# Six-stage transformer block on one core: normalisation, gate and dispatch taken chunk by chunk into the end of the preceding stage

## The reference

```python
x = x + 0.5 * _L0_ffn_ref(_layernorm(x), ...)     # routed attention of top-k tokens, "ffn"
x = x + _L0_attn_ref(_layernorm(x), ...)          # causal attention, 16 heads of 8, "attn"
x = x + 0.5 * _L0_ffn_ref(_layernorm(x), ...)     # "ffn"
x = x + 0.5 * _L1_ffn_ref(_layernorm(x), ...)     # mixture of 8 experts, top 2, "moe"
x = x + _L1_attn_ref(_layernorm(x), ...)          # linear attention with a convolution, "lin"
x = x + 0.5 * _L1_ffn_ref(_layernorm(x), ...)     # "moe"

def _layernorm(x, eps=1e-05):
    return (x - mean(x)) / sqrt(var(x) + eps)

def _L1_ffn_ref(x, ln_w, Wg, bg, ...):
    xn = x * rsqrt(mean(x * x) + finfo.eps) * ln_w
    vals, idx = top_k(xn @ Wg + bg, 2)
    w = softmax(vals)
    # for each expert e: y = (silu(xn @ W1a + b1a) * (xn @ W1b + b1b)) @ W2 + b2
    # out = sum over the token's two experts of w * y
```

## Time and profile before

| what | value |
| --- | --- |
| median of three runs | 1043.1 us (1043.07 to 1043.85) |
| the profiled execution | 1034.16 us, span 1032.4 us |
| mean granted TensorE clock | 0.822 of full speed |
| busy PE, DVE, ACT, POOL | 671.4, 546.3, 388.5, 291.3 us |
| chain that ended last | PE 49%, DVE 23%, issue 7%, POOL 7%, ACT 6%, DMA 6% |
| of it the dispatch (POOL xg L485) | 6% |
| VectorE's scaled rows (L575) | 96 of 345 ns, 25.5 us |
| stage borders in the profile, about | 166, 396, 550, 766 and 818 us |

### The profile page before, as it was taken

The page is one execution under the profiler, slowest core; times in us unless marked ns, Lnnn a source line. Parts: engine busy times, 40 slices in busy tenths (PEclk is TensorE's granted clock), DMA queues, the critical chain, the costliest instruction groups (busy, mean ns, idle before and its releaser), DMA issues.

```text
span 1032.4 us, 13439 instructions
## 1 busy us (share of the span) xinstructions
PE 671.4 (65%) x4584; PEld 489.6 (47%) x4590; DVE 546.3 (53%) x1578; ACT 388.5 (38%) x689; POOL 291.3 (28%) x319
## 2 busy tenths in 40 slices
PE   2069895316999993079894029999715540899991
PEld 1056783211222232056784028999614430799990
DVE  6976758920111118976758404444388860344444
ACT  3053312425999983053311004444303020344440
POOL 2160202201223223060200742333307047133331
PEclk8579997756999997579995559999957855899996
DMA  9600000355510000000000244666220011566743
GB/s 347 231 1 1 1 1 15 81 95 107 67 23 1 2 2 1 0 1 1 1 2 0 85 151 139 211 216 197 89 81 0 1 52 64 194 197 210 218 142 132
DMA packets 40368, 86.74 MB, mean 84 GB/s; under 512 B 5592, under 2 KB 24664, under 8 KB 39784
## 3 DMA queue, kind: packets, MB, share of 16 engines
q1 hardware_dynamic: 35304, 75.53, 25.1%
q0 software_dynamic: 4992, 10.30, 2.8%
HBM read 70.93 MB, written 23.00 MB: 91 GB/s over the span
## 4 chain that ended last, share of the span: by engine, by line
PE 49%; DVE 23%; issue 7%; POOL 7%; ACT 6%; DMA 6%; SPq 3%; POOLq 0%; ACTq 0%; DVEq 0%
PE ps L1654 16%; PE ps L1665 8%; POOL xg L485 6%; PE ps L1568 4%; ACT arena L1255 4%; PE ps L1345 3%; DVE arena L584 2%; DVE arena L589 2%; PE ps L1551 2%; DMA arena<-scr_k 2%; SPq L334 2%; PE ps L1318 2%; DVE stats L514 2%; PE ps L1415 2%; PE ps L1452 1%
## 5 line engine op out<-in xcount | busy, mean ns | idle before, releaser
L845 DVE SCALAR_TENSOR_TENSOR arena<-ps,arena 128x256 f32<-128x256 f32 x184 | 89.1, 484 | 166.1 <-ACT arena L1286 166.1
L1654 PE MATMUL ps<-arena 128*128 128x256 f32 x736 | 170.6, 385 | 2.8 <-issue 1.5
L1255 ACT ACTIVATE arena<-ps 128x512 f32<-128x512 f32 (+3 forms) x192 | 138.4, 826 | 28.4 <-PE ps L1551 27.0
L1654 PEld LDWEIGHTS ps<-arena 128*128 128x128 f32 x736 | 138.2, 193 | 22.5 <-issue 4.0
L1286 ACT ACTIVATE arena<-ps,arena 128x256 f32<-128x256 f32 x184 | 87.5, 476 | 147.7 <-issue 89.9
L492 POOL DMA_INDIRECT yd<-arena x92 | 88.0, 957 | 188.3 <-DVE arena L853 174.2
L485 POOL DMA_INDIRECT xg<-Xn,arena x64 | 61.6, 963 | 106.8 <-DVE arena L781 87.9
L1665 PE MATMUL ps<-arena 128*128 128x128 f32 x736 | 89.8, 274 | 1.4 <-DVE arena L853 1.4
L1665 PEld LDWEIGHTS ps<-arena 128*128 128x128 f32 x736 | 86.0, 192 | 1.8 <-issue 1.7
L1568 PE MATMUL ps<-arena 128*32 128x512 f32 (+3 forms) x768 | 83.5, 507 | 2.4 <-DVE arena L1053 1.6
L474 POOL TENSOR_SCALAR_AFFINE_SELECT arena<-arena 128x512 f32<-128x512 f32 x64 | 40.6, 635 | 140.3 <-ACT arena L1255 140.3
(11 more groups left out here) (243 smaller groups left out, 1188.9 us busy)
## 6 DMA issues: line engine op xcount, KB each, us to landing
arena<-in_wall SPq DMA_DIRECT2D x46, 836.0 KB, 4.9
xg<-in_zeros SPq DMA_DIRECT2D x16, 520.0 KB, 15.8
arena<-xg SPq DMA_DIRECT2D x46, 130.0 KB, 3.9
arena<-yd SPq DMA_DIRECT2D x8, 512.0 KB, 5.6
arena<-scr_q SPq DMA_DIRECT2D x24, 128.0 KB
arena<-scr_k SPq DMA_DIRECT2D x24, 128.0 KB
scr_q<-arena SPq DMA_DIRECT2D x4, 384.0 KB, 6.2
scr_k<-arena SPq DMA_DIRECT2D x4, 384.0 KB, 7.1
```

Source lines behind the costliest of these rows:

```text
L845: nc.vector.scalar_tensor_tensor(out=hT[:, j % 2, f, :], in0=ps[:, 3 + k % 3, 0:TS], scalar=raw[:, slot, EW_BB + f:EW_BB + f + 1], in1=sl[ ...
L1255: nc.scalar.activation(Pa[:, s_ % 3, 2 * u:2 * u + 2, 0:n], ps[:, 2 * w:2 * w + 2, 0:n], ACT.Exp, scale=AD ** -0.5).then_inc(sem("exp", i), 1)
L1654: ins = mm(ps[:, bank, 0:TS], raw[:, slot, w + P * f:w + P * (f + 1)], xTt[:, j % 2, :], start=True, stop=True)
```

## The change

The root chain moves into the loop over chunks. `begin(c, i)` takes the place of `row_stats` and its helpers: statistics of the chunk, variance, ScalarE's root of four columns, the Newton step, and a new column `shift`, minus mean times scale. For the experts the two norms are folded into one root. ScalarE writes the normalised rows as scale times X plus shift, four activations a chunk, and copies chunk c - 1's transposed rows between them. In the experts' stage `begin(c, i)` also calls `pick(i, c - 1)` and `place(i, c - 2)`, and TensorE works in the order transposes, rank, gate of the chunks. After an `ffn` stage, TensorE transposes the next stage's chunk 0 before the last four tiles of the scatter. The PSUM banks of transposes and gates are laid out so that they are free by then, and the router's small tiles move out of the shared arena into the space of wq. SyncE loads the weights of four tiles before it waits for the dispatch. The weighted sum at the end of the experts is spread: ScalarE multiplies the first row of each token, GpSimd the second and adds the two, VectorE adds the sum to X.

```diff
...
+        after_ffn = lambda i: i > 0 and kinds[i - 1] == "ffn"
+        norm_bank = lambda i, c: 2 * c if kinds[i] == "moe" and after_ffn(i) else c
+        gate_bank = lambda i, c: 2 * c + 1 if after_ffn(i) else 4 + c
...
+                def weights_in(j):
+                    slot = (before * NTILE + j) % WSLOT
                     expert = sp.value_load(tab[0:1, NTILE + j:NTILE + j + 1], min_val=0, max_val=E_ - 1)
                     sp.dma_start(raw[:, slot, :], a["wall"][:, bass.ds(expert, 1), :].rearrange("p o w -> p (o w)")
                                  ).then_inc(sem(f"w_in{slot}"), 16)
-                    if j == 0:
-                        sp.wait_ge(*at("dispatched", i, 16 * 2 * NT))
+
+                for j in range(WSLOT):
+                    weights_in(j)
+                sp.wait_ge(*at("dispatched", i, 16 * 2 * NT))
+                for j in range(NTILE):
+                    slot = (before * NTILE + j) % WSLOT
+                    if j >= WSLOT:
+                        sp.wait_ge(*at("y", i, j - WSLOT + 1))
+                        weights_in(j)
...
+                pool.wait_ge(*at("mix", i, 1))
+                for c in range(NC):
+                    ts = slice(4 * c, 4 * c + 4)
+                    pool.wait_ge(sem(f"yf_in{c}"), 16 * (before + 1))
+                    nc.gpsimd.tensor_tensor(yf[:, ts, 1, :], yf[:, ts, 1, :],
+                                            mix[:, ts, 1:2].broadcast_to([P, 4, D]), ALU.mult
+                                            ).then_inc(sem("second", i), 1)
+                    pool.wait_ge(*at("second", i, c + 1))
+                    pool.wait_ge(*at("first", i, c + 1))
+                    nc.gpsimd.tensor_tensor(yf[:, ts, 1, :], yf[:, ts, 1, :], yf[:, ts, 0, :], ALU.add
+                                            ).then_inc(sem("ysum", i), 1)
...
+            def begin(c, i):
+
+                ts = slice(4 * c, 4 * c + 4)
                 for t in range(4 * c, 4 * c + 4):
                     ins = nc.vector.bn_stats(stats[:, t, :], X[:, t, :])
                 link(ins)
                 for t in range(4 * c, 4 * c + 4):
                     ins = nc.vector.bn_aggr(mv[:, t, :], stats[:, t, :])
                 link(ins)
-                if kinds[i] == "attn":
-                    if c == 1:
-                        variance(i, 0)
-                    if c == 2:
-                        inverse_root(i, 0)
-                    if c == 3:
-                        variance(i, 1)
-                        scaled_rows(i, 0)
-                        inverse_root(i, 1)
-                        scaled_rows(i, 1)
-                elif c == NC - 1:
-                    variance(i, None)
-                    inverse_root(i, None)
-                    if kinds[i] == "moe":
-                        root_of_square(i, None)
-                    scaled_rows(i, None)
...
+                mean, v, var, r, w, shift = mv[:, ts, 0], mv[:, ts, 1], rt[:, 0, ts], rt[:, 1, ts], rt[:, 2, ts], rt[:, 3, ts]
+                if kinds[i] == "moe":
+                    ins = nc.vector.tensor_scalar(var, v, 1.0 + RMS_EPS, LN_EPS * RMS_EPS, ALU.mult, ALU.add)
+                else:
+                    ins = nc.vector.tensor_scalar(var, v, LN_EPS, None, ALU.add)
+                ins.then_inc(sem("var"), 1)
+                dve.wait_ge(*at("root", i, c + 1))
+                link(nc.vector.reciprocal(r, w))
                 newton(r, var, w)
+                nc.vector.scalar_tensor_tensor(out=shift, in0=mean, scalar=-1.0, in1=r, op0=ALU.mult, op1=ALU.mult
+                                               ).then_inc(sem("scale"), 1)
                 if kinds[i] == "moe":
...
+                    if c >= 1:
+                        pick(i, c - 1)
+                    if c >= 2:
+                        place(i, c - 2)
...
-                pick(0)
-                pick(1)
-                place(0)
-                pick(2)
-                place(1)
-                pick(3)
-                place(2)
-                place(3)
+                place(i, 2)
+                pick(i, 3)
+                place(i, 3)
...
-                dve.wait_ge(*at("mix", i, 1))
                 for c in range(NC):
                     ts = slice(4 * c, 4 * c + 4)
-                    dve.wait_ge(sem(f"yf_in{c}"), 16 * (before + 1))
-                    link(nc.vector.tensor_tensor(yf[:, ts], yf[:, ts], mix[:, ts].unsqueeze(3).broadcast_to([P, 4, 2, D]),
-                                                 ALU.mult))
+                    dve.wait_ge(*at("ysum", i, c + 1))
                     xs = X[:, ts, :]
-                    link(nc.vector.tensor_tensor(xs, xs, yf[:, ts, 0, :], ALU.add))
                     link(nc.vector.tensor_tensor(xs, xs, yf[:, ts, 1, :], ALU.add))
...
+            def scaled_rows(i, c):
+                ts = slice(4 * c, 4 * c + 4)
+                act.wait_ge(*at("var", i, c + 1))
+                nc.scalar.activation(rt[:, 2, ts], rt[:, 0, ts], ACT.Sqrt).then_inc(sem("root"), 1)
+                act.wait_ge(*at("scale", i, c + 1))
+                for t in range(4 * c, 4 * c + 4):
+                    ins = nc.scalar.activation(Xn[:, t, :], X[:, t, :], ACT.Identity, scale=rt[:, 1, t:t + 1],
+                                               bias=rt[:, 3, t:t + 1])
+                ins.then_inc(sem("xn"), 1)
 
             def layer_norm(i):
+                if i == 0 or kinds[i - 1] != "moe":
+                    preload(ACT.Sqrt)
+                for c in range(NC + 1):
+                    if c < NC:
+                        scaled_rows(i, c)
+                    if c:
+                        transposed(i, c - 1)
...
+                preload(ACT.Sqrt)
+                act.wait_ge(*at("mix", i, 1))
+                for c in range(NC):
+                    act.wait_ge(sem(f"yf_in{c}"), 16 * (before + 1))
+                    for t in range(4 * c, 4 * c + 4):
+                        ins = nc.scalar.activation(yf[:, t, 0, :], yf[:, t, 0, :], ACT.Copy, scale=mix[:, t, 0:1])
+                    ins.then_inc(sem("first", i), 1)
...
+                        if i < last and TB * b + j == NT - 4:
+                            transpose_chunk(i + 1, 0)
...
-                transposes(i)
-                gate(0)
-                gate(1)
-                rank(0)
-                gate(2)
-                rank(1)
-                gate(3)
-                rank(2)
-                rank(3)
+                for c in range(NC):
+                    if c or not after_ffn(i):
+                        transpose_chunk(i, c)
+                    if c:
+                        rank(c - 1)
+                    gate(c)
+                rank(NC - 1)
```

194 lines of the change are left out of this document (76 added, 118 removed).

## The result

The changed kernel takes **1054.6 us** (median of 4 runs, 1053.1 to 1056.4) beside 1043.5 of the kernel before (4 runs): ratio 1.0101, 95% interval 1.0076 to 1.0126. It is 11 us slower, where 1043.4 was forecast with a range that ended at 1047.2. Its profiled execution is 1054.57 us with a span of 1052.8; that of before was 1034.16 with 1032.4. So the two traces differ by 20.4 us and the medians by 11. Each ratio compares the faster runs of both kernels (a run more than 1.5% above the fastest of its kernel is left out), so in the experiments it can differ from the quotient of the medians.

What follows compares the result with a forecast made beforehand. At stage handovers the chain was taken to run through VectorE, and behind the experts' router through GpSimd's stores. Place terms summed to +0.3 us, added to the 1043.1 median: 1043.4 us, range 1038.6 to 1047.2.

Steps and rivals of the forecast that it cites:

- start: Kernel start: the new chain has its logits by about 20, before VectorE's wait for the last weights ends at 21.09; 0.
- feed-forward to attention: Handover into attention: chunked chain starts the last chunk 3.6 us later, memset holds its variance, rows follow; +1.4 us.
- attention to feed-forward: Handover into feed-forward: same chunked chain with a longer memset, everything moving 4.7 us later before rows and logits; +1.7 us.
- feed-forward to experts: First experts' entry: first slots 3.7 us earlier, but GpSimd's stores run out after chunk 0's eight; -1.6 us.
- experts to linear: Experts into linear attention: sums spread over engines, chunked chain, holds beside GpSimd, then ScalarE's rows; -0.8 us.
- linear to experts: Second experts' entry: chunks of 2.05 us, first slots at 834.0, the second slots in time; -0.5 us.
- end: Program end: four chunks of 2.3 us, three meetings of 0.35 and a last sum of 0.9; +0.1 us.
- ScalarE's rows: Normalised rows moved to ScalarE: four take 1.2 us, bounds 1.0 to 1.5, only the last chunk's on the path.
- a wait before each pick: Experts' entries: VectorE waits for the previous chunk's gate behind ScalarE's rows, 3.7 us, or 2.8 for the first gate.
- rival 3: VectorE's two-input SBUF operations stop for whole GpSimd operations: first experts' end 2.7 more, last sums 1.0; +3.7, 1047.1 us; chance 0.20.
- the hold of the variance: Last chunk's variance held until GpSimd's memset ends: 0.70 us entering attention, 2.47 entering feed-forward, where it is else 0.17.
- the start's cover: Kernel start: the wait for the last weights hides the longer chunked chain, with only 1 us to spare.

Runs made afterwards that it cites:

- e6: Changed kernel with the weighted sums of the last experts' stage alone back on VectorE: 1058.7 us, ratio 1.0212.
- e4: Changed kernel with the normalised rows back on VectorE, four behind each chunk's chain, ScalarE keeping only the root: 1072.2 us, ratio 1.0279.
- e8: Changed kernel with ScalarE's copy of chunk c-1's transposes ahead of chunk c's root and rows at the experts' entries: 1059.3 us, ratio 1.0193.
- e1: Kernel before, no edit, run for a second profile: 1040.3 us, ratio 0.9969.
- e3: Changed kernel with the router as before: all transposes, then gates and ranks after the last chunk, picks in one row: 1053.8 us, ratio 1.0109.
- e5: Changed kernel, no edit, run for a second profile and more runs: 1062.4 us, ratio 1.0226.
- e9: Changed kernel with GpSimd's first dispatch store waiting for the slots of all four chunks: 1085.6 us, ratio 1.0387.
- e12: Kernel before with GpSimd's memsets at the attention and feed-forward entries held until the last normalised row: 1042.3 us, ratio 0.9966.
- e13: Changed kernel recombined: batched norm without router, late memsets, last sums on VectorE, copy before rows, picks and ranks behind the last chunk: 1039.2 us, ratio 0.9975.
- e14: Changed kernel, no edit, run again on another chip: 1063.3 us, ratio 1.0222.

## Why the prediction was wrong

The forecast sum was +0.3 us over the places; the same places cost +9.8 in the trace. Term by term:

```
place                        forecast   measured
start                             0       +0.15
feed-forward to attention       +1.4      +1.7
attention to feed-forward       +1.7      +2.95
feed-forward to experts         -1.6       0.0
experts to linear               -0.8      +0.7
linear to experts               -0.5      +0.8
end                             +0.1      +3.5
```

- **The end** is the step that failed most. It counted VectorE's and GpSimd's sums, which did cost 0.3 (17.5 us from the last store to VectorE's last copy before, 17.8 after), and put at nothing what GpSimd does after its last instruction: 3.2 us. The drain was in the trace of before, out of sight because GpSimd had stopped long ahead. e6 shows it: with the last sums on VectorE all 3.5 us come back.
- **ScalarE's rows** were sized from a 0.26 us activation of another tile and a surcharge. Four take 1.65 us and not 1.2, outside the bounds of 1.0 to 1.5. That is 0.45 us; at the first border it is the whole miss of 0.3, as the chunks came 0.1 earlier there. It is part of each other place.
- **Attention to feed-forward**: the rest, 0.9 us, is that the logit matmuls ran at 2.67 us instead of 1.80, at a granted clock of 0.50 throughout. The prediction named such a thing (matmuls after a longer rest of TensorE stay at the lower level) for the attention's first matmuls only, as what could make it wrong, and priced it at nothing; here it took over the 2.94 of the kernel before unchanged.
- **Feed-forward and linear into experts**: the chain of events was right (a wait before each pick, a gap behind the eighth store), the waits were 3.58 and 4.2 us against 2.8 and 3.7, and the gap 2.8 against 1 to 2. So at the first entry the first store came 2.5 us earlier and not 3.7, and the last one not at all. What the prediction did not see is that the wait had a cause that could be taken away: the copy behind the rows on ScalarE (e4, e8).
- **Experts to linear**: rival 3 took place for the first chunk. The 0.4 us for a sum beside GpSimd, read from a group's mean, was 0.8, and four small operations met GpSimd instead of two, 3.0 us in all and not 1.6. The rows add 0.45, and the 0.9 for a root behind ScalarE's products did not come. In sum the place is 1.5 us above the forecast, where rival 3 had 2.7.
- **The median** moved by 11.2. With 9.8 from the places, 1.4 is left. The interiors do not settle it: in the after trace the second feed-forward is 5.3 us longer than before, but 125.4 appears in kernels of both kinds (e1, e3, e5, e9, e12), and so does 127.9 (e12, e13 and the changed kernel). Still, of the feed-forward interiors in profiles of these two kernels alone, none of four before is longer than 125.5 and five of six after are (after, e5, e14: 127.7 to 130.8). That the change makes the longer ones more frequent, at 2.3 to 5.4 us each, is a rival that these few profiles neither show nor rule out.
- **The late completions** are a cost of the change that its own first profile does not have. Where they occur, stores and the stage behind them take about 5 + 5 us more at the second entry, and the kernel's median is 1062 to 1063 instead of 1054.6. The prediction had no term for it, and the trace of before could hardly have given one: there the last rank comes 1.1 us behind its pick, when five stores have begun. The second profile of that kernel (e1) has 2.9 and 4.1 us, so the lateness is not the changed kernel's alone; there it cost nothing, as no store waited for it.

That chunks cost 1.57 us each in front of the last variance was right (pitch 5.86 us forecast 5.90), so was the hold of the variance, and that the start's cover was thin (e4, whose chunks are longer, takes 2.4 us more there).

## What to carry to other kernels

Before work is moved to an engine at a program's end, look at how long that engine needs to close after its last instruction; here the 6.5 us behind GpSimd's last instruction had been covered by VectorE's sums. When a step is cut into chunks, write down for each engine what stands ahead of the next consumer's input: one exchange on ScalarE brought the first store 6.9 us forward and another 3.9. And cut the chain into chunks only where its extra operations are covered by something else: at the three borders without a router one chain over the batch was 1.8 to 4.1 us cheaper.
